# Experts: tokens sorted by expert into DRAM during cross attention, then blocks of 128 rows through one expert each

## The chip, the cores and the metric

The kernel runs on one core of one Trainium2 chip. The metric is the device time of one execution in microseconds (us). The core has TensorE (PE in the profile, with its weight loads as PEld), VectorE (DVE), ScalarE (ACT), GpSimd (POOL) and SyncE (SP), each with its own queue of instructions in order, and 16 DMA engines.

## The reference

A decoder layer over x of 64 sequences, 128 tokens, 128 features, each of its three parts followed by x = layernorm(x + part(x)): causal linear attention with 16 heads, cross attention with 16 heads of 64 over 120 context rows and the 128 rows of x, and a mixture of experts. The last part, cut to what matters:

```
logits = x @ gate_w.T;  scores = softmax(logits)                  # 8 experts
topk_w, topk_i = top_k(scores, 2);  topk_w = topk_w / sum * 2.5
combine = zeros(T, 8).at[arange, topk_i].set(topk_w)
g = silu(einsum('td,edf->etf', x, w_gate)) * einsum('td,edf->etf', x, w_up)   # f = 176
y = einsum('te,etd->td', combine, einsum('etf,efd->etd', g, w_down))
y = y + (silu(x @ sw_gate) * (x @ sw_up)) @ sw_down               # shared MLP, 352 wide
```

Everything is fp32. There are 64 x 128 = 8192 tokens.

## The kernel before

The program is unrolled and has no loops on the chip. Each stage is one block: five functions, one for each queue, that list their instructions in an order written by hand, with semaphores between them (`wait_ge`, `then_inc`). X (128 tokens x 64 sequences x 128 features) stays in SBUF through all stages. A product marked as split (`split_product`, L489 to L491) is three products in the rounded format fp32r: both operands are a high and a low part, and hi x lo, lo x hi and hi x hi are added in PSUM. SP loads the weights of the later stages during linear attention (`LaterWeights.load`).

`linear_attention` takes two sequences per step. `cross_attention` takes two sequences per round, 32 rounds, each with 16 units s = 0 to 15 (a pair of heads for one sequence). A unit s of TensorE is: turn the weights of unit s (four transposes into `ps_T`, L955), the scores of unit s+3 (two split products, `ps_S`), then for even s a `make_G` and for odd s a `make_V` (split products), and every fourth unit a `gang_output` into `ps_O` (L930). The output projection `output` (L919) is at s = 2, the next round's key transposes at s = 4. VectorE takes the maxima of unit s+3 (L786) and the inverse of unit s+2's sums (L792), and copies V, G's low part and the gang's output. ScalarE takes the exponentials of unit s+2 (L728). POOL multiplies unit s+2 by its inverse (`weights`, L653). At s = 3 VectorE adds the residual and takes the moments of the round before; POOL takes their deviation at s = 4 and 5 and normalises each row block at s = 8 and 9 (L645), first into `xnew`, then into X. Ahead of the rounds POOL builds `spread` (L683 to L690) and splits the MLP weights in four operations on 1760 columns (L696, L698).

`experts` works on 16 groups of 512 tokens. The hidden rows of all eight experts and of the shared MLP are 1760, in 14 blocks of up to 128. For every block and group there are a gate product, an up product (each split, 512 columns), one product that spreads the routing weights of the block's expert over its rows (`ps_c`, L1325, for 11 blocks), silu on ScalarE, two products on VectorE, a split of the result into high and low part on ScalarE and POOL (L1161, L1117), and the down projection (split). So every token goes through every expert, and `combine` holds zeros for the six that it did not choose. The routing of a group (a product for the logits, 21 small operations on VectorE over 128 x 32 elements, L1217 to L1240) is written between the blocks. At the end of a group VectorE adds X and takes moments, POOL normalises (L1131 to L1138) and SP stores.

Of the kernel before, what the change touches and what calls it, by code (L numbers as in the profile page):

```python
# [84 lines left out]
def constants(nc, ident, tri):  # L85

    with ExitStack() as stack:
        room = Room(nc, stack, "const")
        filled = room.sem("filled")
        shaped = room.sem("shaped")  # L90
# [3 lines left out]
        def _(pool):  # L94
# [4 lines left out]
                                    pattern=[[-1, P]], channel_multiplier=1).then_inc(shaped, 1)  # L99
            nc.gpsimd.affine_select(out=tri[:], in_=tri[:], compare_op=ALU.is_ge, fill=0.0, base=0,  # L100
                                    pattern=[[1, P]], channel_multiplier=-1).then_inc(shaped, 1)
            pool.wait_ge(shaped, 2)


class LaterWeights:


    def __init__(self, nc, stack, gains, w_q, w_kv, w_out, gate_w, w_gate, w_up, w_down, sw_gate, sw_up, sw_down):
# [5 lines left out]
        self.blocks, self.expert_blocks = -(-FA // P), FE // P  # L114
# [7 lines left out]
        self.down = room.sbuf("down", [P, self.blocks, D])  # L122
        self.gate_part = [room.sbuf(f"gate_{n}", [P, FA], F32R) for n in ("hi", "lo")]
        self.up_part = [room.sbuf(f"up_{n}", [P, FA], F32R) for n in ("hi", "lo")]
        self.spread = room.sbuf("spread", [P, FE], F32R)
        self.attention_loaded, self.gains_loaded = room.sem("attention_loaded"), room.sem("gains_loaded")
        self.gate_loaded, self.mlps_loaded = room.sem("gate_loaded"), room.sem("mlps_loaded")
        self.down_loaded = room.sem("down_loaded")
        self.sources = gains, w_q, w_kv, w_out, gate_w, w_gate, w_up, w_down, sw_gate, sw_up, sw_down

    def load(self, sp):
# [7 lines left out]
        sp.dma_start(self.gw_rows[:], gate_w).then_inc(self.gate_loaded, 16)  # L139
        for n, (w, sw) in enumerate(((w_gate, sw_gate), (w_up, sw_up))):  # L140
# [3 lines left out]
        full, at = self.FS // P, self.expert_blocks  # L144
        sp.dma_start(self.down[:, 0:at, :], w_down.rearrange("e f d -> (e f) d").rearrange("(n p) d -> p n d", p=P)
                     ).then_inc(self.down_loaded, 16)
        sp.dma_start(self.down[:, at:at + full, :], sw_down[0:full * P].rearrange("(n p) d -> p n d", p=P)
                     ).then_inc(self.down_loaded, 16)
        sp.dma_start(self.down[0:self.FS - full * P, at + full, :], sw_down[full * P:self.FS]
                     ).then_inc(self.down_loaded, 16)  # L150


def linear_attention(nc, X, lat, ident, tri, x, weights, biases, later):
# [11 lines left out]
    with ExitStack() as stack:  # L165
# [41 lines left out]
        half_ready, ones_ready = room.sem("half_ready"), room.sem("ones_ready")  # L207
# [46 lines left out]
        def _(pool):  # L254
            nc.gpsimd.memset(half[:], -0.5).then_inc(half_ready, 1)
            nc.gpsimd.memset(ones[:].bitcast(F32), 1.0).then_inc(ones_ready, 1)
            pool.wait_ge(half_ready, 1)
# [163 lines left out]
        def _(pe):  # L421
# [6 lines left out]
            pe.wait_ge(ones_ready, 1)  # L428
# [65 lines left out]
def cross_attention(nc, X, lat, ctx, ident, later):  # L494
# [21 lines left out]
    GANGS = UNITS // GANG  # L516
    with ExitStack() as stack:
# [27 lines left out]
        xnew = room.sbuf("xnew", [P, 2, D])  # L545
# [6 lines left out]
        ones_ready, spread_ready = room.sem("ones_ready"), room.sem("spread_ready")  # L552
# [17 lines left out]
        half_ready, vare_ready, rstd_ready = room.sem("half_ready"), room.sem("vare_ready"), room.sem("rstd_ready")  # L570
        xnew_ready, x2_ready = room.sem("xnew_ready"), room.sem("x2_ready")
# [12 lines left out]
        def _(sp):  # L584
# [8 lines left out]

            load(0, 0)
            load(2, 1)
            for r in range(2, ROUNDS):
                sp.wait_ge(kT_psum, r - 1)
                load(r * 2, r % 2)
            for par in range(2):
                sp.wait_ge(kT_psum, ROUNDS - 1 + par)  # L600
                load(par * 2, par)
            for par in range(2):
                sp.wait_ge(ctx_loaded[par], (ROUNDS // 2 + 1) * 16)
                sp.wait_ge(lat_loaded[par], (ROUNDS // 2 + 1) * 32)

        @block.gpsimd
        def _(pool):
            nc.gpsimd.memset(half[:], -0.5).then_inc(half_ready, 1)
            pool.wait_ge(half_ready, 1)

            def keys_hi(n, par):
                wait_apart(pool, half_ready, (kT_ready, n + 1))
                nc.gpsimd.tensor_copy(kT_part[0][:, par], kT_full[:]).then_inc(kT_hi_ready, 1)
# [6 lines left out]
            def context_deviation(n):  # L620

                wait_apart(pool, half_ready, (cmom_ready, n * 2 + 2))
# [4 lines left out]
            def normalise_context(n, par, u):  # L627
                wait_apart(pool, half_ready, (crstd_ready, n + 1))
# [4 lines left out]
            def deviation(r, u):  # L633

                n = r * 2 + u
                wait_apart(pool, half_ready, (mom_ready, n + 1))
                nc.gpsimd.tensor_scalar(vare[:, u:u + 1], mom[:, u, 1:2], EPS, None, ALU.add).then_inc(vare_ready, 1)
                pool.wait_ge(vare_ready, n + 1)
                nc.gpsimd.tensor_tensor(rstd[:, u:u + 1], vare[:, u:u + 1], half[:, 0:1], ALU.pow).then_inc(rstd_ready, 1)

            def normalise(r, u):

                n = r * 2 + u
                wait_apart(pool, half_ready, (rstd_ready, n + 1))
                nc.gpsimd.tensor_scalar(xnew[:, u, :], hsum[:, u, :], mom[:, u, 0:1], rstd[:, u:u + 1], ALU.subtract,  # L645
                                        ALU.mult).then_inc(xnew_ready, 1)
                wait_apart(pool, half_ready, (xnew_ready, n + 1))
                nc.gpsimd.tensor_copy(X[:, bass.ds(n * D, D)], xnew[:, u, :]).then_inc(x2_ready, 1)
# [7 lines left out]
            def body(r, par):  # L656
                unit = r * UNITS
                for s in range(UNITS):
                    weights(unit + s + 2, (s + 2) % RINGS)
                    if later_round(r) and s in (4, 5):  # L660
                        deviation(r - 1, s - 4)
                    if s == 6:
                        keys_hi(r + 1, 1 - par)
                    if s == 7:
# [754 lines left out]
```

## Time and profile before

| | |
|---|---|
| time, median of 3 runs | 2270.97 us (2267.64 to 2271.44) |
| profiled execution | 2267.62 us |
| its span (first to last instruction) | 2265.6 us |
| mean granted TensorE clock | 0.985 of full speed |
| busy: TensorE, VectorE, ScalarE, POOL | 96%, 70%, 65%, 61% |
| DMA | 33.46 MB, 15 GB/s over the span |

The stages by time from the span's start: linear attention to about 320 us, cross attention to about 1697, experts to the end. The busy share of an engine over the whole span mixes the stages; the rows further down show them apart. A bracket at a row's end says how long the engine was idle just before it and who ended the wait.

### The profile page before, as it was taken

What the parts mean: (1) busy time and instruction counts of PE and PEld (TensorE: products, weight loads), DVE (VectorE), ACT (ScalarE), POOL (GpSimd) and SP (SyncE); (2) the same over time, 40 slices, a digit from 0 to 9 for tenths busy, and PEclk for the clock granted to TensorE, in tenths of its full rate; (3) what the DMA queues carried; (4) which work ended last, traced back from release to release, by engine and by line L of the source; (5) the groups of instructions that cost most, each with busy time, mean ns of one, the idle gap of its engine ahead of it and who ended that gap; (6) DMA issues with size and microseconds to landing.
All of it is one profiled execution on the core that took longest, in us unless ns stands there. A gap on an engine that the chain in (4) does not pass through costs nothing. (4 is left out here: it accounts for less than half of the span.)

```text
span 2265.6 us, 44642 instructions
## 1 busy us (share of the span) xinstructions
PE 2163.8 (96%) x16233; PEld 1841.5 (81%) x16233; DVE 1575.9 (70%) x3455; ACT 1479.8 (65%) x3820; POOL 1386.0 (61%) x1481
## 2 busy tenths in 40 slices
PE   6899967999999999999999999999989999999998
PEld 3455547999999999999999999999977777777776
DVE  3899965666666666666666666666657777777775
ACT  4788845667676666666676766666655665665664
POOL 4788856566565565565665655655654666666666
PEclk9999979999999999999999999999999999999999
DMA  3311110000000000000000000000000000000000
GB/s 93 113 33 33 30 30 5 6 10 6 10 7 6 10 6 6 11 6 6 11 6 10 7 6 10 6 6 10 6 1 1 10 5 10 10 5 10 10 5 14
DMA packets 52794, 33.46 MB, mean 15 GB/s; under 512 B 2968, under 2 KB 50274, under 8 KB 52450
## 3 DMA queue, kind: packets, MB, share of 16 engines
q1 hardware_dynamic: 50174, 26.30, 4.0%
q10 hardware_dynamic: 2404, 4.33, 0.7%
q8 instruction: 131, 2.15, 0.4%
q14 instruction: 85, 0.70, 0.1%
HBM read 22.22 MB, written 8.39 MB: 14 GB/s over the span
## 5 line engine op out<-in xcount | busy, mean ns | idle before, releaser
L653 POOL TENSOR_TENSOR x_prob<-x_prob,x_inv 128x496 f32<-128x496 f32 x514 | 521.7, 1015 | 546.9 <-DVE x_inv L792 546.9
L728 ACT ACTIVATE x_prob<-x_ps_S,x_nmax 128x248 f32<-128x248 f32 x1028 | 473.2, 468 | 130.4 <-DVE x_nmax L786 130.3
L786 DVE TENSOR_REDUCE x_nmax<-x_ps_S 128x2 f32<-128x496 f32 x515 | 345.5, 671 | 181.3 <-PE x_ps_S L491 181.1
L736 ACT COPY x_probT<-x_ps_T 124x512 f32<-124x512 f32 x512 | 300.7, 587 | 225.0 <-PE x_ps_T L955 225.0
L1117 POOL TENSOR_TENSOR e_hidden_lo<-e_hidden,e_hidden_hi 128x512 fp32r<-128x512 f32 x224 | 291.8, 1306 | 196.6 <-ACT e_hidden_hi L1161 195.7
L489 PE MATMUL x_ps_S<-x_kT_lo,x_G_hi 128*128 128x248 f32 x1030 | 329.6, 320 | 0.0
L955 PE MATMUL x_ps_T<-ident,x_prob 128*124 128x128 f32 x2048 | 315.1, 276 | 11.3 <-POOL x_prob L653 11.3
L955 PEld LDWEIGHTS x_ps_T<-ident,x_prob 128*124 128x124 f32 x2048 | 237.8, 139 | 71.7 <-POOL x_prob L653 29.2
L490 PE MATMUL x_ps_S<-x_kT_hi,x_G_lo 128*128 128x248 f32 x1030 | 287.3, 279 | 0.0
L491 PE MATMUL x_ps_S<-x_kT_hi,x_G_hi 128*128 128x248 f32 x1030 | 286.7, 278 | 0.0
L772 DVE TENSOR_TENSOR x_G_lo<-x_ps_G,x_G_hi 128x512 fp32r<-128x512 f32 x259 | 178.8, 690 | 129.2 <-ACT x_G_hi L722 129.1
L930 PE MATMUL x_ps_O<-x_probT,x_V 124*64 124x128 f32 x4096 | 251.8, 276 | 0.2 <-ACT x_probT L736 0.2
L930 PEld LDWEIGHTS x_ps_O<-x_probT,x_V 124*64 124x64 f32 x4096 | 220.9, 137 | 18.9 <-issue 5.1
L1172 ACT ACTIVATE e_silu<-e_ps_gate 128x512 f32<-128x512 f32 x224 | 134.5, 601 | 154.5 <-PE e_ps_gate L491 149.0
L722 ACT CAST x_G_hi<-x_ps_G 128x512 fp32r<-128x512 f32 x259 | 152.0, 587 | 91.6 <-PE x_ps_G L491 91.4
L728 ACT ACTIVATION_READ_ACCUMULATOR x_prob<-x_ps_S,x_nmax 128x1 f32 x1028 | 206.8, 201 | 0.0
L490 PEld LDWEIGHTS x_ps_S<-x_kT_hi,x_G_lo 128*128 128x128 f32 x1030 | 196.3, 191 | 0.0
L489 PEld LDWEIGHTS x_ps_S<-x_kT_lo,x_G_hi 128*128 128x128 f32 x1030 | 195.4, 190 | 0.0
L491 PEld LDWEIGHTS x_ps_S<-x_kT_hi,x_G_hi 128*128 128x128 f32 x1030 | 194.8, 189 | 0.0
L1257 DVE TENSOR_TENSOR e_act_up<-e_silu,e_ps_up 128x512 f32<-128x512 f32 x176 | 120.3, 684 | 90.2 <-PE e_ps_up L491 52.8
L778 DVE COPY x_V<-x_ps_V 124x512 f32<-124x512 f32 x259 | 176.6, 682 | 1.8 <-PE x_ps_V L491 1.8
L1161 ACT CAST e_hidden_hi<-e_hidden 128x512 fp32r<-128x512 f32 x224 | 137.4, 613 | 26.7 <-DVE e_hidden L1263 25.9
(199 smaller groups left out, 5135.3 us busy)
## 6 DMA issues: line engine op xcount, KB each, us to landing
x_nk<-latents SPq DMA_DIRECT2D x34, 124.0 KB
lin_x_rows<-in_x SPq DMA_DIRECT2D x32, 128.0 KB, 2.4
latents<-lin_nlat SPq DMA_DIRECT2D x32, 128.0 KB, 1.8
out_dram<-e_result SPq DMA_DIRECT2D x16, 256.0 KB, 2.2
x_nk<-in_ctx SPq DMA_DIRECT2D x34, 120.0 KB, 2.1
w_wkv<-in_L_xattn_Wkv SPq DMA_DIRECT2D x1, 1024.0 KB, 6.1
w_rows<-in_L_ffn_w_gate SPq DMA_DIRECT2D x1, 704.0 KB, 5.8
w_rows<-in_L_ffn_w_up SPq DMA_DIRECT2D x1, 704.0 KB, 6.2
```

What stands on the lines that cost most here:

```text
L489: nc.tensor.matmul(out, stationary[0], moving[1], start=first, stop=False)
L490: nc.tensor.matmul(out, stationary[1], moving[0], start=False, stop=False)
L491: return nc.tensor.matmul(out, stationary[0], moving[0], start=False, stop=last)
L653: nc.gpsimd.tensor_tensor(prob[:, k], prob[:, k], inv[:, k].unsqueeze(2).broadcast_to([P, 2, K]), ALU.mult).then_inc(prob_ready, 1)
L728: nc.scalar.activation(prob[:, k, h, :], ps_S[:, n % BANKS, h * K:(h + 1) * K], ACT.Exp, bias=nmax[:, k, h:h + 1], accum_out=total[:, k, h ...
L736: nc.scalar.copy(probT[0:KT, s % (2 * GANG)], ps_T[0:KT, s % 2, :]).then_inc(probT_ready, 1)
L772: nc.vector.tensor_tensor(G_part[1][:, pair].rearrange("p h u q -> p (h u q)"), ps_G[:], G_part[0][:, pair].bitcast(F32).rearrange("p h u ...
L778: nc.vector.tensor_copy(V[:, hf, u, tile, :], ps_V[0:KT, :]).then_inc(V_ready, 1)
L786: nc.vector.tensor_reduce(nmax[:, k, :], ps_S[:, n % BANKS, 0:2 * K].rearrange("p (h k) -> p h k", h=2), AX, ALU.max, negate=True).then_in ...
L930: last = nc.tensor.matmul(ps_O[h * DH:(h + 1) * DH, k * S:(k + 1) * S], V[:, j // 4, u, tile, (j % 4 * 2 + h) * DH:(j % 4 * 2 + h + 1) * D ...
L955: last = nc.tensor.transpose(ps_T[0:KT, s % 2, at:at + S], prob[:, s % RINGS, h, tile * KT:(tile + 1) * KT], ident[:])
L1117: nc.gpsimd.tensor_tensor(hidden_part[1][0:rows, n % RING, :], hidden[0:rows, n % 2, :], hidden_part[0][0:rows, n % RING, :].bitcast(F32), ...
```

## The change

Three things change together.

Routing moves into cross attention. One round behind the attention, TensorE turns the normalised rows of the two sequences (`turn_rows`, ahead of unit 7; it waits for POOL's normalised rows `staged`), ScalarE copies them out, and SP stores them turned in DRAM (`turned_rows`). TensorE takes the logits (`logits`, ahead of unit 8) into a part of `ps_O`, so the gang output at s = 8 waits until VectorE has read them. VectorE takes 25 small operations per round (`route`), in the groups that `ROUTE` gives; ranks within each expert come from a product with a triangle of ones (`ranks`, at s = 14) and a running count `base`. POOL normalises both rows at s = 5 and 6, copies them to X, makes a second copy with the row's number and its routing weight beside it, and at s = 0 to 3 of the round after next sends the rows with four indirect DMAs of 128 rows (132 floats each) to their expert's region in DRAM (`sorted_rows`). There are two batches of 32 sequences. After the last round this work stands alone.

The weights: no `spread`; the splitting of the MLP weights into ten pieces between the units of round 0; TensorE waits for all small constants (`set_ready`, 29) before its first product. Down projections are in plain fp32, not split.

The experts' stage becomes a loop over 142 blocks (71 a batch, a fixed number; the regions' ends are padded) of 128 rows that share one expert. VectorE works out from the counts which expert and which rows a block has; SP and TensorE each read that number into a register for each block (`value_load`). Results go back to DRAM by an indirect DMA from POOL for each block (`sorted_results`), in the order of the tokens. The shared MLP is computed in 16 groups of 512 tokens from `turned_rows`, two groups ahead of the loop and 14 in eight pieces each between the first 112 blocks. The first batch's eight groups are loaded back, added and normalised during the second batch, the second batch's after the loop.

The diff, cut to its core (comments are mine; in VectorE's loop of the last stage the guards on t are left out):

```diff
 def cross_attention(...)            # POOL
-                    if later_round(r) and s in (4, 5):
-                        deviation(r - 1, s - 4)
-                    if s == 6:
+                    if s < 4 and r > 1:
+                        scatter(r - 2, s // 2, s % 2)
+                    if s == 4 and r:
+                        deviation(r - 1)
+                    if s in (5, 6) and r:
+                        normalise(r - 1, s - 5)
+                    if s == 7:
                         keys_hi(r + 1, 1 - par)
...
+                    if s == 9 and r:
+                        keep(r - 1)
+                    if s == 10 and r:
+                        twin(r - 1)
...
+                    if s < 10 and r == 0:
+                        split_weights(s // 5, s % 5)
+            def scatter(n, c, u):
+                pool.wait_ge(twin_ready, n * 2 + 2)
+                pool.wait_ge(routed, (n + 1) * STEPS)
+                nc.gpsimd.indirect_dma_start(slots.rows, bass.IndirectOffsetOnAxis(slot[:, n % 2, c, u:u + 1], 0),
+                                             staged[:, n % 2, c, u, :], None).then_inc(slots.scattered[n % 2], 16)
+            # VectorE, at the end of a unit
+                    if r and s in ROUTE:
+                        route(r - 1, *ROUTE[s])
+            ROUTE = {8: (0, 2), 10: (2, 6), 11: (6, 11), 12: (11, 16), 13: (16, 20), 15: (20, 25)}
+            # route: each step k begins with
+                    wait(dve, routed, n * STEPS + k)
+            # TensorE
+            pe.wait_ge(set_ready, SETS)
+            def turn_rows(n):
+                pe.wait_ge(staged_ready, n * 2 + 2)
+                pe.wait_ge(outT_ready, min((n + 1) * GANGS + 1, ROUNDS * GANGS))
+                for u in range(2):
+                    last = nc.tensor.transpose(ps_O[:, u * S:(u + 1) * S], staged[:, n % 2, 0, u, 0:D], ident[:])
+                    if s == 7 and r:
+                        turn_rows(r - 1)
+                    if s == 8 and r:
+                        logits(r - 1)
...
                     if s % GANG == 0 and unit + s:
+                        if s == 8 and r:
+                            pe.wait_ge(shifted_ready, r)
+                        if s == 0 and r > 1:
+                            pe.wait_ge(routed, (r - 2) * STEPS + 22)
                         gang_output(r * GANGS + s // GANG - 1)
+                    if s == 14 and r:
+                        ranks(r - 1)
 def experts(...)
+    TOTAL = BATCHES * BLOCKS
+    RING = 6
+    SENT = 3
+            def load_rows(i):                                            # SP
+                wait(sp, sent[(i - RING) % SENT], ((i - RING) // SENT + 1) * 16)
+                row = sp.value_load(entry(row_of, i), min_val=0, max_val=BATCHES * BATCH_ROWS - P)
+                sp.dma_start(x_rows[:, i % RING, :], slots.rows[bass.ds(row, P), :]).then_inc(rows_loaded[i % RING], 16)
+            def scatter(i):                                              # POOL
+                pool.wait_ge(y_ready, i + 1)
+                nc.gpsimd.indirect_dma_start(slots.results, bass.IndirectOffsetOnAxis(x_rows[:, i % RING, D:D + 1]...),
+                                             y[:, i % SENT, :], None).then_inc(sent[i % SENT], 16)
+            for t in range(TOTAL + 4):                                   # TensorE
+                if t < TOTAL:
+                    turn_rows(t)        # waits rows_loaded, lo_ready t
+                    expert[t] = pe.value_load(entry(expert_of, t), min_val=0, max_val=EXPERTS - 1)
+                if 0 <= t - 1 < TOTAL:
+                    gate_up(t - 1, expert[t - 1])     # one split product, 352 columns
+                g, k = shared_at(t)
+                if g is not None:
+                    shared(g, k)
+                if 0 <= t - 2 < TOTAL:
+                    turn_hidden(t - 2)
+                if 0 <= t - 3 < TOTAL:
+                    project_down(t - 3, expert.pop(t - 3))
+            for t in range(TOTAL + 4):                                   # VectorE
+                lo(t); product(t - 1); take(t - 3)    # take: ps_y to y, waits sent of block t - 6
+            sent_after(sp, TOTAL)                                        # SP, after the loop
+            for g in range(BACK, GROUPS):
+                load_back(g)
+                if g > BACK:
+                    store(g - 1)
```

## Rows read from the trace of the kernel before

**Rows 1.** The page: busy us, share of the span and instructions of each engine.
```profile
PE 2163.8 (96%) x16233; PEld 1841.5 (81%) x16233; DVE 1575.9 (70%) x3455; ACT 1479.8 (65%) x3820; POOL 1386.0 (61%) x1481
```

**Rows 2.** Busy time of PE, PEld, DVE, ACT, POOL; clock, DMA: two stages.
```profile
370.00:1686.00 1316.00, 1315.76 (x12559) 1225.76 (x12559) 869.37 (x1995) 890.07 (x2789) 761.35 (x948) 1.00 0.03 8
...
1710.00:2256.00 546.00, 544.57 (x2473) 430.17 (x2471) 409.32 (x897) 327.69 (x553) 357.44 (x314) 1.00 0.03 8
```

**Rows 3.** Waits in cross attention, 480 to 1600: total us, times, longest.
```profile
PEld x_ps_T L955 <- POOL x_prob L653: 14.9, 81, 0.2
```

**Rows 4.** Instructions of a tile: ns min/median/max, first and last start.
```profile
L782 DVE COPY x_outT<-x_ps_O x128: 690/692/693, 372.2 to 1686.6; 128x512 f32<-128x512 f32 x128
...
L489 PE MATMUL e_ps_gate<-e_xT_lo,w_gate_hi x224: 388/395/795, 1704.3 to 2249.3; 128*128 128x512 f32 x112
```

**Rows 5.** TensorE in order of time: start, us, instruction; units 7 and 8.
```profile
1580.47 0.60 PE L955 MATMUL x_ps_T<-ident,x_prob 128*124 128x128 f32 x4
...
1584.24 1.97 PE L930 MATMUL x_ps_O<-x_probT,x_V 124*64 124x128 f32 x32
```

**Rows 6.** POOL in order of time in the same round.
```profile
1580.79 1.02 POOL L653 TENSOR_TENSOR x_prob<-x_prob,x_inv 128x496 f32<-128x496 f32 x1
```

**Rows 7.** POOL's groups in the expert stage: count, busy us, mean ns.
```profile
L1138 POOL TENSOR_SCALAR e_result<-e_hsum,e_mom,e_rstd 128x128 f32<-128x128 f32 x51 | 41.5, 813 | 0.0
L1133 POOL TENSOR_TENSOR e_rstd<-e_vare,e_half 128x4 f32<-128x4 f32 x13 | 13.5, 1039 | 1.1
L1131 POOL TENSOR_SCALAR e_vare<-e_mom 128x4 f32<-128x4 f32 x13 | 3.1, 235 | 0.0
```

**Rows 8.** VectorE in order of time in the same round.
```profile
1580.56 0.15 DVE L792 RECIPROCAL x_inv<-x_total 128x2 f32<-128x2 f32 x1
...
1584.38 0.15 DVE L792 RECIPROCAL x_inv<-x_total 128x2 f32<-128x2 f32 x1
```

**Rows 9.** VectorE, then POOL, in order of time in the expert stage.
```profile
1935.27 1.09 DVE L1220 TENSOR_TENSOR e_equal<-e_score,e_col 128x32 f32<-128x32 f32 x1
...
1940.02 0.20 DVE L1228 TENSOR_TENSOR e_equal<-e_rest,e_col 128x32 f32<-128x32 f32 x1
...
1935.01 2.55 POOL L1117 TENSOR_TENSOR e_hidden_lo<-e_hidden,e_hidden_hi 128x512 fp32r<-128x512 f32 x2
```

**Rows 10.** TensorE, then POOL, in order of time at the start of cross attention.
```profile
334.97 0.46 PE L489 MATMUL x_ps_V<-x_wv_lo,x_kT_hi 128*124 128x512 f32 x1 [1.64 <-POOL x_kT_lo L617]
...
362.29 1.11 PE L955 MATMUL x_ps_T<-ident,x_prob 128*124 128x128 f32 x4 [7.68 <-POOL x_prob L653]
...
336.80 1.59 POOL L630 TENSOR_SCALAR x_nk<-x_nk,x_cmom,x_crstd 120x128 f32<-120x128 f32 x2 [0.18 <-POOL x_crstd L625]
```

**Rows 11.** TensorE in order of time: 16 fp32 products, two 512-column products.
```profile
1567.08 3.73 PE L919 MATMUL x_ps_V<-w_wo,x_outT 128*128 128x128 f32 x32
...
2250.23 0.39 PE L490 MATMUL e_ps_up<-e_xT_hi,w_up_lo 128*96 128x512 f32 x1
...
2250.46 0.39 PE L491 MATMUL e_ps_up<-e_xT_hi,w_up_hi 128*96 128x512 f32 x1
```

**Rows 12.** DMA issues: KB each, median us from issue to landing.
```profile
latents<-lin_nlat SPq DMA_DIRECT2D x32, 128.0 KB, 1.8
out_dram<-e_result SPq DMA_DIRECT2D x16, 256.0 KB, 2.2
...
lin_w_rows<-in_L_attn_Wq SPq DMA_DIRECT2D x1, 64.0 KB, 1.9
...
lin_b_v<-in_L_attn_bv ACTq DMA_DIRECT2D x1, 64.0 KB, 2.9
```

**Rows 13.** Busy time and granted clock near linear attention's end, then TensorE there.
```profile
296.00:300.00 4.00, 2.31 (x7) 0.96 (x6) 3.97 (x10) 2.87 (x6) 3.05 (x4) 1.00 0.00 0
300.00:304.00 4.00, 2.57 (x7) 2.03 (x8) 3.96 (x6) 1.29 (x4) 3.92 (x3) 0.67 0.12 35
...
301.43 1.19 PE L464 MATMUL lin_ps_vy<-lin_w,lin_turned 128*128 128x128 f32 x4 [3.02 <-ACT lin_turned L322]
```

More of the change, by code:

```diff
@@ L700, in _ @@
             rounds(pool, body)
+            last = ROUNDS - 1
+            for k in range(4):
+                scatter(last - 1, k // 2, k % 2)
+            deviation(last)
             for u in range(2):
-                deviation(ROUNDS - 1, u)
-                normalise(ROUNDS - 1, u)
-            pool.wait_ge(part_ready, 4)
-            pool.wait_ge(spread_ready, 1)
+                normalise(last, u)
+            keep(last)
+            twin(last)
+            for k in range(4):
+                scatter(last, k // 2, k % 2)
@@ L1007, in _ @@
             output(ROUNDS - 1)
+            turn_rows(ROUNDS - 1)
+            logits(ROUNDS - 1)
+            ranks(ROUNDS - 1)
 GROUP = 4
@@ new lines, in experts @@
+        empty_id = room.sbuf("empty_id", [P, CLOSERS], mybir.dt.uint32)
+        numbers = {}
+        NUMBERS = 8 + 2 * BATCHES
+        for name, shape in (("order", [EXPERTS]), ("start", [BATCHES, EXPERTS]), ("level", [MOST]), ("block", [BLOCKS]),
+                            ("block_row", [BATCHES, BLOCKS])):
+            numbers[name] = (room.sbuf(f"{name}_i", [1] + shape, I32), room.sbuf(f"{name}_f", [1] + shape))
+        count, needed, until, skip = (room.sbuf(n, [1, BATCHES, EXPERTS]) for n in ("count", "needed", "until", "skip"))
@@ L1141, in _ @@
-            run(pool, step)
+            for name, pattern in (("order", [[1, EXPERTS]]), ("level", [[P, MOST]]), ("block", [[1, BLOCKS]])):
+                nc.gpsimd.iota(numbers[name][0][:], pattern, base=0, channel_multiplier=0).then_inc(numbers_ready, 1)
+            for n in range(BATCHES):
+                for name, pattern in (("start", [[REGION, EXPERTS]]), ("block_row", [[P, BLOCKS]])):
+                    nc.gpsimd.iota(numbers[name][0][:, n], pattern, base=n * BATCH_ROWS, channel_multiplier=0
+                                   ).then_inc(numbers_ready, 1)
@@ L1143, in _ @@
+            deviation(GROUPS - 1)
+            for k in range(2):
+                normalise(GROUPS - 1, k)
         @block.scalar
         def _(act):
[L1145 to L1153 removed]
@@ new lines, in normalise @@
+            def normalise(g, k):
+                dve.wait_ge(rstd_ready, g + 1)
+                wait(dve, stored[g % 2], g // 2 * 16)
+                v.tensor_scalar(result[:, g % 2, k, :], hsum[:, g % 2, k, :], mom[:, g % 2, k, 0:1],
+                                rstd[:, g % 2, k:k + 1], ALU.subtract, ALU.mult).then_inc(result_ready[1], 1)
+            start, level, order, number, block_row = (numbers[n][1] for n in ("start", "level", "order", "block", "block_row"))
+            v.tensor_copy(end_of[:], slots.base[0:1]).then_inc(table_ready, 1)
@@ new lines, in turn_hidden, with project_down @@
+            def turn_hidden(i):
+                pe.wait_ge(hidden_ready, i + 1)
+                wait(pe, hT_ready, i)
+                for n in range(2):
+                    at = n * P
+                    last = nc.tensor.transpose(ps_h[0:HALF, at:at + P], hidden[:, i % 2, n * HALF:(n + 1) * HALF], ident[:])
+                last.then_inc(h_psum, 1)
+            def project_down(i, e):
+                pe.wait_ge(hT_ready, i + 1)
+                wait(pe, y_ready, i)
+                for n in range(2):
+                    last = nc.tensor.matmul(ps_y[:, 0:D], hT[:, i % 2, n * P:(n + 1) * P],
+                                            later.down[:, bass.ds(e, 1), n, :].rearrange("p o d -> p (o d)"),
+                                            start=(n == 0), stop=(n == 1))
+                last.then_inc(y_psum, 1)
```

976 lines of the change are left out of this document (606 added, 370 removed).

## The prediction

> **What bounds the kernel now.** I read the page first, to find the busiest engine, then the busy times of each stage, then the waits of each stage, then stretches in order of time. TensorE is busy for 96% of the span [rows 1], and by stage it is full in the two stages that the change touches: 1315.8 of 1316 us in cross attention and 544.6 of 546 us in the experts, at full clock [rows 2]. In cross attention it hardly waits: 14.9 us for POOL's weights over 27 rounds [rows 3]. So time added to TensorE's queue in cross attention, work or wait, is added to the end, and the expert stage is worth what its matmuls take. The copy of a gang's output starts 128 times, first at 372.2 and last at 1686.6 us [rows 4]: 127 steps of 10.35 us, 41.4 us for a round of 16 units.
>
> **What the change takes away.** The expert stage lasts from 1704.3, its first gate product [rows 4], to the end at 2265.6, 561 us. Its six 512-column products per hidden block, three of the down projection and the spread products go; only two of eight experts are computed per token.
>
> **Cross attention, part by part.** The routing moves here: 31 of 32 rounds carry it, while TensorE is full.
>
> (a) The wait at unit 7. TensorE's `turn_rows` stands ahead of unit 7's transposes and needs both rows normalised. POOL normalises the second at unit 6 behind `weights(unit+8)`. Now unit 7's transposes start at 1580.47 [rows 5], while POOL begins that `weights` at 1580.79 (1.02 us) [rows 6], and a normalisation of this shape takes 0.81 us [rows 7]: 1582.65. TensorE waits 2.15 us, with everything queued behind, and then does two transposes (0.12 each, four in 0.60 with the end of the last [rows 5]): 2.4 us.
>
> (b) The wait at unit 8. The gang output now waits until VectorE has shifted the logits. VectorE gets there only behind that unit's maxima and its inverse, which starts at 1584.38 [rows 8]; two operations of 0.22 us each bring it to 1584.95, where the gang output starts at 1584.24 now [rows 5]. With the logits' own matmuls (0.25): 0.9 us.
>
> (c) `ranks`: four small matmuls, 0.3 us.
>
> (d) The 23 other routing operations on VectorE, in groups of 4 or 5 behind the inverse of units 10 to 13 and 15. Alone each costs 0.19 us and follows the last by 0.22, so a group is 1 us. But the trace shows such an operation, `e_equal` with both inputs in SBUF, at 1.09 us: it starts at 1935.27 while POOL is in a two-input operation that began at 1935.01, two of them in 2.55 us, and it ends with the first of them; the same shape without POOL beside it takes 0.20 [rows 9]. In cross attention POOL starts `weights` (1.01 us) 0.23 us after each inverse [rows 6, 8], just where the groups stand. So every group holds until POOL is through, and they last 1.5, 2.0, 2.1, 1.9 and 1.7 us. I laid the engines side by side from unit 7 on with the durations of these rows: VectorE's own work is 1.3 us for a unit, 1.9 with an output copy, and TensorE's 1.84. Through units 10 to 15 VectorE has 8.4 us of its own and 9.2 of routing, 17.6, for TensorE's 13.0. Its lead absorbs the first 2 us of the difference; then the maxima come late, the exponentials, inverses and POOL's weights behind them, and TensorE waits 0.3 us (at 14, for G_lo), 1.35 (at 15) and 0.95 (at the next 0) for POOL. Then the long units 0 and 2 let VectorE catch up. (c) and (d) together: 2.9 us.
>
> The Trainium skill (SBUF — State Buffer, SBUF: two separate sides) says that VectorE's two-input operations and POOL's take one pair of ports as an exclusive lock, and the loser is blocked for the whole instruction. The trace agrees (1.09 against 0.20 us). Without that rule the sum would be 102 us less.
>
> Together 2.4 + 0.9 + 2.9 = 6.2, and with 0.3 for POOL's scatters delaying `weights`, 6.5 us a round, 31 times: +202 us. From below: without (d)'s stretching 3.3 us, 102. From above 8 us, 248.
>
> (e) Start-up: the pieces of the weights' splitting no longer stand in one lump that has TensorE waiting 7.68 us at 362.29 and then running at half clock [rows 10], worth about 9 us, of which POOL, nearly full in round 0, takes back 3. But TensorE's first product, at 334.97, now waits for constants that POOL makes only after its last context normalisation (to 338.4) [rows 10], and some 29 small fills: 341. It cancels: 0 (from −6 to +6).
>
> **Between the stages.** The last round's routing is bare. From the last output copy at 1686.6 [rows 4]: the copy 0.7, the output projection 3.8 [rows 11], sum and moments 1.6, deviation 1.3, two normalisations 1.6, two copies 0.7: 1696.3. Then turn, logits, 25 routing steps of 0.22 and ranks (1702), four scatters of 1.2: 1707. Then POOL makes numbers, VectorE a chain of about 18 table operations (on up to 1136 elements on one partition, 10 to 12 us) with the products of the first shared group between them; TensorE needs the shared groups 0 and 1 done, 6.9 us each and waiting in between. The block loop starts at about 1736 (1728 to 1745) on the present axis.
>
> **The block loop.** 2 x 71 = 142 blocks, fixed when built. TensorE per block: one transpose 0.2; three products with 352 columns, 0.45 (0.23 for 512 [rows 11]); two transposes 0.2; two fp32 matmuls at 3.73/16 = 0.23 [rows 11], 0.47. Pieces of the shared MLP in the first 112 steps: 6 x 0.23 and 12 x 0.23 for a group, over 8 steps, 0.5; with the waits between its halves I take 0.75. A bare sum would be 2.07 us a step, 1.32 without shared pieces.
>
> But `load_rows(i)` waits for the scatter of block i−6, and TensorE's `turn_rows(i)` has `project_down(i−3)` queued behind it. So three steps hold one whole chain: 3T = w + L. w is a step of TensorE from the rows' arrival to the end of `project_down`: 2.07 + register load 0.9 + drain 0.2 = 3.2 (2.4 without shared). L: VectorE's copy 0.35 (0.15 for its shortest operation [rows 8], and 128 columns), the scatter's issue on POOL, its landing, a wake-up 0.1, the register load on SP 0.9, and the load. Transfers: 1.8 us for the latents' store, 1.9 for 64 KB, up to 2.9 [rows 12]. No row shows an indirect issue: from 0.23 (POOL's smallest [rows 7]) to 2.6 (two of its large ones [rows 9]); I take 1.2, like one, since it handles 128 rows. Nor a register load: from 0.15 [rows 8] to 1.9 [rows 12], the middle, 0.9. L = 0.35 + 1.2 + 1.8 + 0.1 + 0.9 + 1.9 = 6.25. T = 3.15 with shared pieces, 2.9 without: 112 x 3.15 + 29 x 2.9 = 436 us. From the lower ends T is about 2.3 (325), from the upper ones 4.5 (640).
>
> The Trainium skill (DMA: Bandwidth & Descriptors, Anatomy of one DMA — SWDGE) gives about 2.0 us + bytes/436e3 for a whole DMA issued by POOL, 2.15 for 64 KB; the nearest row, SP's 1.9 us, agrees as far as it goes. With it in place of my 3.0, T would be 2.85 and the sum 40 us less. A page's floor for a register load, about 0.6 us (same title, Latency and other measured facts), has no row here.
>
> Then drain: three short steps, copy, scatter, landing, 7.5 us. **The tail**: eight groups of the second batch only then. Per group POOL adds the pair (1.3 [rows 9]), takes the deviation (0.24 + 1.04) and normalises twice (0.81 each [rows 7]): 4.3 us with the waits, 34; two 256 KB loads ahead 3.5 (2.2 for one such store [rows 12]) and the last group's sum and store 4.5: 42.
>
> **Sum**: 1736 + 202 + 436 + 7.5 + 42 = 2423.5 us span. The profiled execution took 2267.6 for a span of 2265.6, the median of the runs is 3.4 above it: 2429.
>
> **Rivals.** (1) The routing hides under TensorE as far as VectorE goes (no lock, or VectorE's lead is enough): 2429 − 102 = 2327. For it: VectorE is idle a third of cross attention [rows 2]. Against: the operation of 1.09 us [rows 9]. Chance 0.13. (2) TensorE, with gaps in every step, falls to half its clock in the block loop: its work is 4.0 us a step and the step 4.4 (3.3 without shared): 589 us, 2582. The row that could speak for it shows 0.67 of full clock only after 3 us without work, while 2.3 busy of 4 us kept 1.00 [rows 13]; the gaps here are under 1.5 us. The Trainium skill (TensorE: Matmul & The Clock Gate, What's actually happening) also has the idle array fall to 1.2 GHz. Chance 0.10. (3) Faster: the chain L is short enough for TensorE's own work to pace the loop. That needs L under about 3.9 us; the loop is 112 x 2.07 + 29 x 1.32 = 270 us and the time 2263, and less with (1). It decides at T of 1.95 with my cross attention, at 2.65 with rival 1's. For it: transfers of 1.8 us; against: two of them in sequence already fill the 3.9. Chance 0.19. The forecast has the rest, 0.58, with its own range 2340 to 2520.
>
> **The numbers.** The measurement tells 0.2%, about 4.5 us, from no change. Range 2285 to 2570: rival 1 with somewhat quicker steps below, T near 3.9 above. Faster 0.18, same 0.02, slower 0.80.
>
> **What would show it.** A round of cross attention at 48 us against 41.4, with TensorE waiting for POOL's `staged` rows ahead of unit 7 (2.1 us) and for weights at 15 and 0; routing operations of about 1 us on VectorE; blocks 3.1 us apart, TensorE idle for the DMA of `x_rows`, SP waiting for scatters; the tail paced by POOL. Wrong if the indirect issue costs POOL much more than 2 us (it would then also hold `weights`), or if the blocks come every 2 us.

## The result, and the profile after

The changed kernel takes 2476.8 us in the median (2474.95 to 2486.3, four runs); on the same chip the kernel before took 2269.3. The ratio is 1.092 (95% interval 1.089 to 1.095): 9% slower. Predicted were 2429 us, in a range of 2285 to 2570. The profiled execution has a span of 2476.1 us at a mean clock of 0.935.

The page of the kernel after, busy time of each engine; TensorE was at 96% in [rows 1]:

```profile
PE 2076.3 (84%) x16149; PEld 1785.3 (72%) x16149; DVE 1595.9 (64%) x4024; ACT 1329.8 (54%) x3814; POOL 1362.6 (55%) x1515
```

TensorE is busy for only 88 us less, in a span 210 us longer. The same view by stage as [rows 2], after: cross attention, change-over, the block loop with shared pieces, the loop without them, the tail (the last three columns are granted clock, DMA share and GB/s):

```profile
375.00:1885.00 1510.00, 1397.05 (x12846) 1287.27 (x12842) 1073.25 (x2768) 908.43 (x2846) 884.39 (x1044) 0.98 0.05 15
1885.00:1939.00 54.00, 25.92 (x126) 20.45 (x127) 20.56 (x59) 7.30 (x12) 16.61 (x31) 0.72 0.24 70
1939.00:2300.00 361.00, 284.29 (x1682) 236.57 (x1681) 153.88 (x443) 127.68 (x386) 127.94 (x129) 0.95 0.21 61
2300.00:2393.00 93.00, 65.76 (x299) 54.45 (x299) 37.18 (x134) 26.79 (x89) 46.19 (x49) 0.73 0.25 71
2393.00:2476.00 83.00, 6.80 (x31) 5.17 (x30) 22.70 (x96) 1.99 (x6) 39.65 (x45) 0.52 0.28 81
```

Two tiles give the borders of the stages, as [rows 4] did: the copies of the gang outputs, and the first transpose of each block (ns min/median/max, first and last start):

```profile
L895 DVE COPY x_outT<-x_ps_O x128: 677/692/693, 375.3 to 1884.7; 128x512 f32<-128x512 f32 x128
...
L1707 PE MATMUL e_ps_x<-ident,e_x_rows x142: 270/327/477, 1939.0 to 2393.4; 128*128 128x128 f32 x142
```

127 steps in 1509.4 us are 47.54 us a round against 41.40, so cross attention costs 195 us more, and it begins 3.1 us later. (That start, 375.3 here, lies between 369.0 and 375.8 us in the traces of the kernels below, whose code up to there is this one's, so the 3.1 us mean little.) The blocks come 454.4 / 141 = 3.22 us apart. From the last block's start to the end are 82.7 us. Between the last gang copy and the first block lie 54.3 us.

| step | predicted | measured |
|---|---|---|
| start-up | 0 | +3 |
| cross attention | +202 | +195 |
| from the last gang copy to the block loop | 49.4 | 54.3 |
| start of the block loop | 1938 | 1939 |
| block loop | 436 (3.09 a step) | 454.4 (3.22) |
| drain and tail | 49.5 | 82.7 |
| span | 2423.5 | 2476.1 |

**Waits in cross attention.** The waits of the kernel after, 480 to 1800 us, 27 rounds (total us, times, longest), where [rows 3] had 14.9 us in all:

```profile
PEld x_ps_O L1146 <- POOL w_rows L695: 59.5, 27, 2.2
PEld x_ps_T L1185 <- POOL x_prob L738: 48.0, 56, 1.0
...
PEld x_ps_O L1127 <- DVE x_shifted L970: 16.6, 27, 0.6
```

Per round TensorE's weight loads (PEld) wait 2.2 us for the rows to be turned, 1.8 for POOL's weights (0.55 before) and 0.6 for the shifted logits.

**One round at unit 7.** TensorE, then POOL, in order of time; L695 writes the normalised rows, L738 is `weights`:

```profile
1571.72 0.69 PE L1146 MATMUL x_ps_O<-ident,w_rows 128*128 128x128 f32 x2 [2.00 <-POOL w_rows L695]
1572.20 1.06 PE L1185 MATMUL x_ps_T<-ident,x_prob 128*124 128x128 f32 x4
...
1575.39 0.51 PE L1153 MATMUL x_ps_O<-x_gwT,w_rows 128*128 128x8 f32 x4
...
1569.03 0.81 POOL L695 TENSOR_SCALAR w_rows<-x_hsum,x_mom,x_rstd 128x128 f32<-128x128 f32 x1
1569.88 1.01 POOL L738 TENSOR_TENSOR x_prob<-x_prob,x_inv 128x496 f32<-128x496 f32 x1
1570.87 0.79 POOL L695 TENSOR_SCALAR w_rows<-x_hsum,x_mom,x_rstd 128x128 f32<-128x128 f32 x1
```

The second normalisation stands behind `weights` and TensorE waits 2.00 us for it, as predicted. What I had not predicted comes after it: from unit 7's transposes to the logits TensorE takes 3.19 us. The granted clock (third column from the end) of that stretch and of the next one says why. The last row is the same stretch one round later:

```profile
1571.70:1575.20 3.50, 3.48 (x15) 3.30 (x16) 0.63 (x2) 0.96 (x2) 0.00 (x0) 0.51 0.24 74
1575.40:1578.40 3.00, 2.59 (x25) 2.39 (x25) 2.14 (x9) 2.06 (x7) 2.02 (x3) 1.00 0.14 42
...
1620.10:1623.60 3.50, 3.50 (x29) 3.36 (x30) 1.92 (x7) 2.18 (x7) 1.10 (x2) 1.00 0.25 77
```

TensorE was full until the wait, and after 2 us without work it runs 3.5 us at 0.51, its lower level of 1.2 GHz, before it has 2.4 GHz again. But not in every round: the wait is 2.00 us in all 31, and the clock fell behind it in 20 of them; in the other 11, as in the one from 1620.1, it stayed at 1.00, and the way from the transposes to the logits took 1.83 us. A round with the fall lasts 48.4 us, one without it 46.8: 1.6 us for each fall, 1.0 a round on average. Why it fell after some of these equal waits and not after others is open.

**One turn of the block loop**, the kernel after in order of time: VectorE's copy of a result, POOL's scatter, SP's row loads (two issues in the row, the second at its end), the next block's transpose:

```profile
2101.62 0.29 DVE L1581 COPY e_y<-e_ps_y 128x128 f32<-128x128 f32 x1 [1.19 <-PE e_ps_y L1731]
2102.19 0.96 POOL L1459 DMA_INDIRECT sorted_results<-e_y,e_x_rows  x1 [1.88 <-DVE e_y L1581]
2102.32 3.76 SPq L1371 DMA_DIRECT2D e_x_rows<-sorted_rows  x2
...
2104.86 0.33 PE L1707 MATMUL e_ps_x<-ident,e_x_rows 128*128 128x128 f32 x1 [0.45 <-DMA e_x_rows<-sorted_rows]
```

The second load is issued about 2105.7, 3.5 us after its scatter's start; the load of 2102.32 is used at 2104.86, 2.5 us later. With the copy and a gap, L, the part of the chain outside TensorE, is 0.3 + 0.3 + 3.5 + 2.5 = 6.6 us in this turn (6.25 predicted). Over the whole loop the medians are lower: 3.2 us from a scatter's start to the issue that waits for it, and 2.3 from an issue to its block's transpose.

### The profile page after: what moved, and what is told of

It is laid out like the page before. It is cut to its first block and busy times, and to the rows that moved or that the text cites. A ratio compares the mean times of both kernels' runs of the same rounds, so it can differ in the third digit from the quotient of the medians.

```text
span 2476.1 us, 47892 instructions
## 1 busy us (share of the span) xinstructions
PE 2076.3 (84%) x16149; PEld 1785.3 (72%) x16149; DVE 1595.9 (64%) x4024; ACT 1329.8 (54%) x3814; POOL 1362.6 (55%) x1515
## 5 line engine op out<-in xcount | busy, mean ns | idle before, releaser
L738 POOL TENSOR_TENSOR x_prob<-x_prob,x_inv 128x496 f32<-128x496 f32 x514 | 521.3, 1014 | 614.8 <-DVE x_inv L905 612.0
L1185 PE MATMUL x_ps_T<-ident,x_prob 128*124 128x128 f32 x2048 | 325.5, 282 | 40.0 <-POOL x_prob L738 40.0
L510 PE MATMUL x_ps_S<-x_kT_lo,x_G_hi 128*128 128x248 f32 x1030 | 335.8, 326 | 0.0
L1459 POOL DMA_INDIRECT sorted_results<-e_y,e_x_rows x142 | 145.5, 1024 | 306.8 <-DVE e_y L1581 301.6
L512 PE MATMUL x_ps_S<-x_kT_hi,x_G_hi 128*128 128x248 f32 x1030 | 291.9, 283 | 0.0
L511 PEld LDWEIGHTS x_ps_S<-x_kT_hi,x_G_lo 128*128 128x128 f32 x1030 | 201.6, 196 | 0.0
L510 PEld LDWEIGHTS x_ps_S<-x_kT_lo,x_G_hi 128*128 128x128 f32 x1030 | 200.5, 195 | 0.0
L512 PEld LDWEIGHTS x_ps_S<-x_kT_hi,x_G_hi 128*128 128x128 f32 x1030 | 199.9, 194 | 0.0
L714 POOL DMA_INDIRECT sorted_rows<-w_rows,x_slot x128 | 132.3, 1033 | 32.6 <-issue 23.7
L510 PE MATMUL x_ps_G<-x_kT_lo,x_M_hi 128*128 128x256 f32 x518 | 146.4, 283 | 0.4 <-DVE x_G_lo L885 0.4
L511 PE MATMUL x_ps_G<-x_kT_hi,x_M_lo 128*128 128x256 f32 x518 | 146.2, 282 | 0.0
```

Source lines behind the costliest of these rows:

```text
L510: nc.tensor.matmul(out, stationary[0], moving[1], start=first, stop=False)
L511: nc.tensor.matmul(out, stationary[1], moving[0], start=False, stop=False)
L512: return nc.tensor.matmul(out, stationary[0], moving[0], start=False, stop=last)
L738: nc.gpsimd.tensor_tensor(prob[:, k], prob[:, k], inv[:, k].unsqueeze(2).broadcast_to([P, 2, K]), ALU.mult).then_inc(prob_ready, 1)
L1185: last = nc.tensor.transpose(ps_T[0:KT, s % 2, at:at + S], prob[:, s % RINGS, h, tile * KT:(tile + 1) * KT], ident[:])
L1459: nc.gpsimd.indirect_dma_start(slots.results, bass.IndirectOffsetOnAxis(x_rows[:, i % RING, D:D + 1].bitcast(mybir.dt.uint32), 0), y[:, i ...
```

## The experiments

Times are medians. The changed kernel, 2476.8, was not timed again beside them; the kernel before was, on the chip of each group (2272.0, 2273.3 and 2267.9), so a quarter of a per cent between groups means nothing.

| run | edit | median us | against before |
|---|---|---|---|
| e1_tail | order of loads in the tail | 2451.4 | 1.079 (1.077 to 1.082) |
| e2_norm | normalise earlier | 2382.4 | 1.050 (1.048 to 1.052) |
| e3_route | routing ahead of the reciprocal | 2441.1 | 1.075 (1.072 to 1.078) |
| e4_ring | nine slots | 2368.1 | 1.044 (1.041 to 1.046) |
| e5_all | these four | 2204.3 | 0.970 (0.968 to 0.971) |
| e6_const | nine slots, fixed experts | 2347.2 | 1.034 (1.032 to 1.035) |
| e7_tail_dve | e5_all, VectorE normalises | 2202.2 | 0.969 (0.967 to 0.971) |
| e8_ring5 | five slots | 2736.2 | 1.207 (1.203 to 1.210) |
| e9_ring7 | seven slots | 2378.0 | 1.049 (1.046 to 1.052) |

**e1_tail**

```diff
+            load_back(BACK)
             for g in range(BACK, GROUPS):
-                load_back(g)
+                if g + 1 < GROUPS:
+                    load_back(g + 1)
                 if g > BACK:
                     store(g - 1)
```

> Only SP's order in the tail of the expert stage changes: the loads of a group stand one group ahead of the store that they stood behind. Theory A (the tail is one serial chain of load, sum, normalise, store, because SP's next load stands behind the last store; 9.23 us a group): seven groups go to POOL's own pace of about 4.5 to 5 us, 30 us less in all, all of it in the last 83 us. Theory B (the transfers themselves pace it: 4.6 us for a group's two loads and 2.2 for its store, 6.8 us): 17 us less. Theory C (order does not matter): no change.

In the kernel after a group of the tail is one chain. SP, then POOL, in order of time:

```profile
2433.11 0.38 SPq L1395 DMA_DIRECT2D out_dram<-e_result  x1
2433.53 1.10 SPq L1388 DMA_DIRECT2D e_back<-sorted_results  x2
2442.53 0.38 SPq L1395 DMA_DIRECT2D out_dram<-e_result  x1
...
2437.94 1.26 POOL L1466 TENSOR_TENSOR e_back<-e_back 128x512 f32<-128x512 f32 x1 [4.85 <-DMA e_back<-sorted_results]
2439.17 0.24 POOL L1473 TENSOR_SCALAR e_vare<-e_mom 128x4 f32<-128x4 f32 x1
2439.49 1.33 POOL L1475 TENSOR_TENSOR e_rstd<-e_vare,e_half 128x4 f32<-128x4 f32 x1
2440.92 1.58 POOL L1481 TENSOR_SCALAR e_result<-e_hsum,e_mom,e_rstd 128x128 f32<-128x128 f32 x2
```

The load is issued right behind a store, lands, POOL sums, normalises, and only then comes the store, with the next load behind it. With the new order POOL has no wait left (e1_tail, POOL):

```profile
2430.15 1.26 POOL L1468 TENSOR_TENSOR e_back<-e_back 128x512 f32<-128x512 f32 x1
...
2433.14 1.58 POOL L1483 TENSOR_SCALAR e_result<-e_hsum,e_mom,e_rstd 128x128 f32<-128x128 f32 x2
2434.73 1.26 POOL L1468 TENSOR_TENSOR e_back<-e_back 128x512 f32<-128x512 f32 x1
```

4.58 us a group instead of 9.2. The last block starts at 2401.0 there, the span is 2454.4: 53.4 us of tail instead of 82.7, 29 us less. Theory A. (Its block loop took 462 us against 454, which hides part of that in the whole time. The loop's code is the same in both; e2_norm and e3_route, which leave it alone too, took 456 and 460, so a difference under 8 us in the loop means nothing.)

**e2_norm**

```diff
                     if s == 4 and r:
                         deviation(r - 1)
-                    if s in (5, 6) and r:
-                        normalise(r - 1, s - 5)
+                        for u in range(2):
+                            normalise(r - 1, u)
```

> POOL's two normalisations of the rows to be routed stand at unit 4 behind the deviation, in POOL's idle time, and no longer at units 5 and 6 with the weights of unit 8 between them. Theory A (unit 7's wait of 2.0 us is this order, and the half clock of TensorE after it, 1.6 us more, follows from the wait): 3.6 us off each of 31 rounds, 110 us less; the products after turn_rows take 0.11 us each again. Theory B (the wait goes but the half clock comes from something else, the transposes of routing or the copy of ScalarE): 62 us less. Theory C (POOL's weights come late instead and TensorE waits for them): under 30 us less.

Its gang copies start from 374.2 to 1785.3: 44.44 us a round, 3.1 less, 98 us in the stage, between A and B but near A. TensorE at unit 7 of e2_norm:

```profile
1536.14 0.38 PE L1146 MATMUL x_ps_O<-ident,w_rows 128*128 128x128 f32 x2
1536.36 0.60 PE L1185 MATMUL x_ps_T<-ident,x_prob 128*124 128x128 f32 x4
...
1538.17 0.59 PE L1153 MATMUL x_ps_O<-x_gwT,w_rows 128*128 128x8 f32 x4
```

The wait is gone, and with it the half clock: 1.81 us from the transposes to the logits, not 3.19, and in none of the 31 rounds did the clock fall. So the half clock came from the wait. The rounds give the price of each: 44.6 us without the wait, 46.8 with it at full clock, 48.4 with it and the fall. The wait cost 2.15 us in 31 rounds, the half clock 1.6 in 20 of them, 67 + 32 = 99 us, where 98 went. That is why theory A's 3.6 us a round, which took a fall in every round, was too much. The waits for POOL's weights are as before the edit (47.9 us).

**e3_route**

```diff
+                    if r and s in ROUTE:
+                        route(r - 1, *ROUTE[s])
                     inverse(unit + s + 2, (s + 2) % RINGS)
                     if s == 7:
                         context_moments(r + 2, par)
-                    if r and s in ROUTE:
-                        route(r - 1, *ROUTE[s])
```

> Each group of routing operations stands ahead of the unit's reciprocal on VectorE and no longer behind it, so that it runs while POOL waits for that reciprocal. Same operations, same number. Theory A (VectorE's operations of 0.8 to 1.1 us are held by POOL's weights, and TensorE's waits for weights, 1.2 us a round above those of the kernel before, come from that): the operations fall to about 0.2 us, 37 us less. Theory B (the operations fall to 0.2 us, but VectorE had lead enough, and TensorE's waits have another origin): within 5 us of no change. Theory C (the reciprocal and so POOL's weights come later by the group's 1 us, which TensorE feels): up to 30 us more.

One such operation of the kernel after beside POOL's weights; then its tile `x_equal` (ns min/median/max) in the kernel after, and in e3_route:

```profile
1584.34 0.82 DVE L980 TENSOR_TENSOR x_equal<-x_score,x_col 128x16 f32<-128x16 f32 x1
...
1584.11 1.01 POOL L738 TENSOR_TENSOR x_prob<-x_prob,x_inv 128x496 f32<-128x496 f32 x1 [0.47 <-DVE x_inv L905]
```

```profile
L980 DVE TENSOR_TENSOR x_equal<-x_score,x_col x32: 174/820/826, 436.3 to 1896.8; 128x16 f32<-128x16 f32 x32
```

```profile
L980 DVE TENSOR_TENSOR x_equal<-x_score,x_col x32: 174/174/177, 435.3 to 1854.0; 128x16 f32<-128x16 f32 x32
```

Same instruction, same size: 0.82 us beside POOL's `weights`, ending as that ends, and 0.17 without. Five of the 25 routing operations of a round are held this way in the kernel after, at 0.7 to 1.0 us, and none in e3_route; together the 25 fall from 7.8 to 4.2 us (480 to 1800 us). The shortest of the 32 in the kernel after is the last round's, where POOL has no weights. The stage falls to 46.22 us a round, 42 us less, and TensorE's waits for weights in e3_route, 26 rounds, are those of the kernel before again:

```profile
PEld x_ps_T L1185 <- POOL x_prob L738: 14.6, 28, 0.6
```

Theory A.

**e4_ring, e9_ring7, e8_ring5**

```diff
-    RING = 6
+    RING = 9        # e9_ring7: 7, e8_ring5: 5
```

> Nine slots for the loaded rows of the block loop where there were six; nothing else. Theory A (three steps hold one whole chain of project, copy, scatter, landing, register load, row load, 3T = w + L with T at 3.22 us; with nine slots six steps hold it, and TensorE's own work with its register load paces the loop): T falls to 2.6 us with shared pieces and 2.0 without, 105 us less. Theory B (the indirect scatters or the row loads are paced by the transfers or by POOL's issue, not by the ring): T stays above 3 us, under 20 us less. Theory C (register loads on SP and TensorE with the waits between engines pace it): T about 2.8 to 2.9, 50 us less.

> Seven slots. Theory A (the same law): four steps hold 9.66 us, 2.42 each, which is no longer above the 2.49 us that nine slots gave; so nearly the whole gain of e4_ring comes with the first slot: 2370 to 2385 us. Theory B (smoothing): a third of it, 2440.

> Five slots in the block loop where the changed kernel has six and e4_ring nine. Theory A (the law of the prediction: RING - 3 steps hold one chain of w + L, which the 3.22 us of six slots put at 9.66 us): two steps hold it, 4.83 us a block, 681 us for the loop, 227 us more than the changed kernel, 2703. If TensorE falls to half clock in the longer gaps, w grows by up to 2 us and the loop to 820. Theory B (the step is set by POOL's issue, SP's issues or the transfers, each under 3.3 us, and the slots only smooth it): under 60 us more.

The first transpose of each block, in e4_ring, e9_ring7 and e8_ring5 in turn:

```profile
L1707 PE MATMUL e_ps_x<-ident,e_x_rows x142: 270/274/448, 1932.2 to 2283.1; 128*128 128x128 f32 x142
```

```profile
L1707 PE MATMUL e_ps_x<-ident,e_x_rows x142: 270/274/444, 1933.0 to 2297.9; 128*128 128x128 f32 x142
```

```profile
L1707 PE MATMUL e_ps_x<-ident,e_x_rows x142: 270/421/477, 1934.8 to 2649.2; 128*128 128x128 f32 x142
```

5, 6, 7 and 9 slots give 5.07, 3.22, 2.59 and 2.49 us a block. The law (slots − 3) T = w + L, with the sum of 9.66 us from six slots, gives 4.83 for five, 2.42 for seven, and 1.61 for nine, which TensorE can't follow. So the chain through the slots set the step (theory A in all three runs), and one slot more brings 90 of the 104 us in the loop. With seven slots the law's 2.42 is already under the 2.49 of nine. TensorE's waits for loaded rows, 1950 to 2250 us, say the same: 89.4 us with five slots, 36.4 with six, 8.6 with seven and none with nine. Six and seven:

```profile
PEld e_ps_x L1707 <- DMA e_x_rows<-sorted_rows: 36.4, 34, 2.7
PEld e_ps_x L1707 <- DMA e_x_rows<-sorted_rows: 8.6, 13, 2.5
```

With five slots 2 x 5.07 = 10.1 us is 0.5 above the sum. TensorE is at half clock half of the time there (e8_ring5, the loop), and its part w, from a block's transpose to the copy of the result of three blocks before, is 3.7 us in the median against 3.0, over the 112 steps with shared pieces. That the half clock makes this difference is likely, not shown:

```profile
1935.00:2500.00 565.00, 376.67 (x1662) 314.88 (x1662) 154.74 (x438) 129.11 (x382) 122.80 (x125) 0.74 0.13 38
```

The whole gain of nine slots is as expected, its parts are not: 2.51 us a block with shared pieces (2.6 expected) and 2.41 without (2.0). In the last 29 blocks TensorE has work for 53 of 70 us, at 0.80 of its clock:

```profile
2213.30:2283.10 69.80, 53.21 (x293) 45.46 (x290) 35.87 (x133) 25.32 (x87) 48.51 (x50) 0.80 0.35 97
```

So nine slots take the chain out of the step, but that TensorE's own work then sets it is not shown.

**e6_const**

```diff
-                    expert[t] = pe.value_load(entry(expert_of, t), min_val=0, max_val=EXPERTS - 1)
+                    expert[t] = t // 9 % EXPERTS
```

> Nine slots as in e4_ring (2368 us), and TensorE does not load the expert's number from the table but takes expert t // 9 mod 8 for block t, written into the program; so the products use the wrong weights, of the same shapes, and 142 register loads of TensorE go. Theory A (with nine slots TensorE is the pacer, and the gap of 0.5 to 0.7 us ahead of a block's first gate product, which the trace ends by nothing it shows, is that load): a block falls from 2.49 to about 2.0 us, 60 to 70 us less. Theory B (the loop is paced by VectorE, POOL or SP by now, and the gap is cover for them): under 15 us less.

21 us less than e4_ring, between theory A's 60 and theory B's 15: neither. The loop takes 328.0 us against 350.9, 2.33 us a block. I had read the length of one gap and not how many there are. The wait of e4_ring ahead of its first gate products, 1950 to 2250 us, some 120 blocks (total us, times, longest):

```profile
PEld e_ps_gu L510 <- issue: 21.7, 36, 0.9
```

36 gaps, 0.18 us a block; ahead of the other blocks' products the trace has no gap, probably as the load is done while TensorE still works. In e6_const this wait is gone (0.2 us in the same stretch), and 0.16 us a block with it. What sets the rest of the 2.33 us was not taken further.

**e5_all**, the edits of e1 to e4 in one kernel.

> The four edits of the runs e1_tail, e2_norm, e3_route and e4_ring together. Alone they gave 25, 94, 36 and 109 us below the changed kernel's 2476.8. Theory A (four separate places, each on the path that sets the end): the gains add, 2213 us, 2.5% faster than the kernel before. Theory B (they share something, such as POOL's time in cross attention or TensorE's clock): 2250 or more, within a per cent of the kernel before.

2204.3 us: theory A, the gains add (2213 from the sum; the 9 us beyond it are not explained). The kernel is 3.0% faster than the one before. Its cross attention, then its loop, then its tail:

```profile
375.00:1745.00 1370.00, 1355.09 (x12837) 1252.45 (x12835) 978.70 (x2767) 899.43 (x2846) 883.34 (x1042) 1.00 0.05 16
1800.00:2147.00 347.00, 304.46 (x1977) 261.99 (x1977) 186.93 (x576) 151.05 (x475) 175.65 (x177) 0.97 0.29 83
2147.00:2200.00 53.00, 5.13 (x34) 3.88 (x32) 22.81 (x97) 2.25 (x8) 40.01 (x46) 0.59 0.44 126
```

TensorE is full again in cross attention (1355 of 1370 us at full clock), at 43.2 us a round: routing's own share is 1.8 us, 56 us in all. It is still at 0.97 in the loop and idle in the tail.

**e7_tail_dve**: as e5_all, and in the tail `normalise(g, k)` stands on VectorE for k = 0 to 3 and no longer on POOL for two of them.

> As e5_all, and in the tail VectorE normalises all four rows of a group where POOL took two of them (VectorE is idle 2 of 4.6 us there, and one of its normalisations takes 0.32 us against POOL's 0.79). Theory A (POOL's queue of 1.26 + 1.57 + 1.58 us paces the tail once the loads stand ahead): 1.6 us less for each of seven groups, 11 us below e5_all. Theory B (the loads, 4.6 us from issue to sum, with two groups of buffers, pace it then): at most 5 us less.

2202.2 us, no difference to e5_all that this can measure; the tail is 52.4 us against 52.9. Theory B. POOL in e7_tail_dve:

```profile
2177.87 1.26 POOL L1468 TENSOR_TENSOR e_back<-e_back 128x512 f32<-128x512 f32 x1 [0.53 <-DMA e_back<-sorted_results]
...
2184.32 1.26 POOL L1468 TENSOR_TENSOR e_back<-e_back 128x512 f32<-128x512 f32 x1 [3.87 <-DMA e_back<-sorted_results]
...
2187.44 1.26 POOL L1468 TENSOR_TENSOR e_back<-e_back 128x512 f32<-128x512 f32 x1 [0.24 <-DMA e_back<-sorted_results]
```

Groups now come in pairs, 9.57 us for two: a group's load is 4 us from its issue to the sum, it is issued right behind an earlier group's store, and there are two buffers. In e5_all POOL's own work filled just that time: its sums come every 4.5 us, hardly waiting.

## Why the prediction was right

The time is 2% above the forecast, inside its own range, and each stage grew by what it named, but for the tail, where it had the order of the work wrong. Two terms of cross attention were off in ways that partly cancel; the loop and the tail were too small.

**Cross attention, +195 for +202.** (a) The wait for the second normalisation is 2.0 us where 2.15 was predicted, the transposes 0.22 to 0.48 for 0.25. The step lacked what can follow such a wait, a stretch at half clock: 1.6 us in 20 of 31 rounds, 32 us in all (e2_norm has none of it). [rows 13] had shown the same after a wait of 3.02 us; I used it for the block loop alone. (b) was 0.6 us of wait and 0.4 of matmuls, for 0.9. (d) was too large: the lock is there, with 0.7 to 1.0 us for an operation that it holds, but it cost TensorE 1.3 us a round (e3_route), not 2.6; VectorE's lead seems to have absorbed more than the 2 us that I gave it. So +1.0 for the half clock and −1.3 met, and the right sum is partly luck. Rival 1, no cost of the lock, was wrong too, as 42 us were real. It was also priced wrong: the stretching was 2.6 us of the working's round, 81 us, and taking 102 away removed `ranks` and the scatters' delay with it. It should have stood at 2348.

The Trainium skill (SBUF — State Buffer, SBUF: two separate sides) says that a VectorE operation with two inputs in SBUF and a GpSimd operation lock each other out of one shared pair of ports for the whole instruction. The trace agrees, with 0.82 against 0.17 us for one and the same operation.

**Between the stages**: 54.3 us for 49.4. These 5 us, the 3 of the start-up and the 7 that cross attention fell short make 1939 for 1938. The mean clock of the change-over is 0.72, which was not in the working; what the clock cost there was not tested.

**The block loop, 454 for 436.** The law 3T = w + L held, tested from both sides (e8_ring5, e9_ring7). 3T is 9.66 against the 9.45 and 8.7 of the working. With shared pieces: 3.23 us a step for 3.15 (block 112 starts at 2301.3). Without: 92.1 / 29 = 3.18 for 2.9. There TensorE ran at 0.73 of its clock, and w fell from 3.0 to 2.6 us in the median, where the working had it fall by 0.8. Rival 2 put the half clock on every step; it came in those 29, and less with the others (mean clock 0.95).

The scatter's issue took 1.02 us (1.2 predicted), the result's copy 0.29 (0.35) and a gap behind it 0.3 (0), the row load 2.5 in the turn shown (1.9). Issue, landing, wake-up and register load were 4.0 us of the working, the wake-up's 0.1 from no row, and 3.5 in that turn. Rival 3 needed L under 3.9 us; it is 6.6, of which 3.5 are the scatter's way from its start to SP's next issue and 2.5 the row load.

**The tail, 83 for 49.5**, the largest miss. The step costed POOL's work per group, 4.3 us, as if the loads were always ahead; the order of SP's queue, `load_back(g)` and then `store(g − 1)`, makes each group one chain of 9.2 us. The rule that I had stated for the loop, what is queued behind the waiting instruction, was not applied to SP here. With the order mended the tail is 53.4, near the 49.5 of the working (e1_tail).

**Start-up**: +3 for 0, within its bounds and within what the runs differ by there.

## What to carry to other kernels

A ring of buffers with a round trip through DRAM in it has a law, (slots − steps queued between) x step = work + latency: write it down, and the number of slots from which the chain no longer sets the step falls out. Here it was seven, not six, for 90 us. A wait on TensorE is to be priced with the half-clock stretch that can follow it, here in two rounds of three, and an order of two engines by hand can remove both for nothing: all the edits that turned 9% slower into 3% faster moved lines or changed one number. Small VectorE operations belong where POOL is waiting for VectorE, ahead of the result that releases it.

## What the runs showed of the hardware

- After 2.0 us without work TensorE, full until then, had about half of its clock for some 3.5 us in 20 of 31 rounds, 1.6 us each time; in the other 11 rounds the same wait left it at full clock.
- An operation of VectorE with two inputs in SBUF took 0.82 us beside a two-input operation of POOL, 0.17 without (`x_equal`, the kernel after and e3_route).
- Issuing an indirect DMA of 128 rows holds POOL for 1.02 us in the mean; from its start to SP's issue of the load that waited for it are at least 2.9 us, 3.2 in the median (the kernel after).
- A register load per block ahead of TensorE's products cost 0.16 us a block (e6_const), where one gap in the trace is 0.6 us in the mean: only a third of the blocks show it.
- Two loads of 256 KB take 3.9 to 4.4 us from their first issue to the operation that waits for them (e7_tail_dve, the kernel after), where one store of that size took 2.2 [rows 12].
